# A mixture of experts in f32 with weights loaded once per expert, in place of f16 pairs loaded per block

## The chip, the core and the metric

The kernel runs on one core of one Trainium2 chip. The metric is the device time of one execution in microseconds; the median over three runs is what kernels are compared by. A profile is one execution of its own.

## What is computed

Sixteen sequences of 64 tokens (D = 256) pass through seven blocks, each with a residual sum: cross-attention to 16 x 256 context rows, self-attention, a mean over eight experts, cross-attention again, a diagonal state-space layer, and then a layer of its own attention and a mixture of eight experts. The change touches that mixture:

```python
h = h + moe(rms_norm(h, norm2_w), router_w, router_b, W1, b1, W2, b2, W3, b3)
...
logits = x @ router_w + router_b
topv, topi = jax.lax.top_k(logits, TOP_K)          # TOP_K = 2
topw = jax.nn.softmax(topv, axis=-1)
h1 = jnp.einsum('bsd,edf->ebsf', x, W1) + b1       # 8 x 256 x 1024
h2 = jnp.einsum('bsd,edf->ebsf', x, W2) + b2
h = h2 * jax.nn.silu(h1)
eo = jnp.einsum('ebsf,efd->ebsd', h, W3) + b3      # 8 x 1024 x 256
out = jnp.einsum('bse,ebsd->bsd', comb, eo)
```

All inputs are f32.

## The kernel before

Every engine has its own hand-written program, and they wait for each other on semaphores. The stages follow one another in the order ln, xa0, sa, ffn, xa1, ssm, rope, la, moe. The cross-attentions (`cross`, 16 steps and 4 to drain) keep K, V and scores of one sequence each; `inner` (sa and la) runs over 8 tiles of 128 tokens with 4 steps to drain. x, its normed copy and its transpose stay in SBUF. The weights of the stages lie in one buffer, `arena`, which the expert stage later uses as a ring of three slots (`ring`).

**Splitting the experts' weights.** A f32 value is kept as a pair of f16, high and low part. The 8 experts have 96 pieces of 128x512. For each, SP loads the piece (L401), POOL copies it to f16 (L1249) and subtracts that copy from the piece (L1250), and SP stores both parts in the DRAM tensor `w_parts` (L407, `pass_piece`). `split_piece` stands in POOL's steps of sa, ffn, xa1 and la, two pieces a step (one in most steps of la). In xa1, SP passes two pieces and then loads the context of the sequence after next (`load_context`, L372), in one queue.

**Tokens.** In la each normed tile (DVE, L1662) is split in the same way: ACT writes the high part (L1101), POOL the low part (L1316). DVE's norm of the next tile waits for `row_lo`. The router (L1807 to L1849) sorts the 2048 pairs of token and expert into 23 blocks of 128 rows, so that every block has one expert, `owner[b]`; spare blocks get the last one. POOL scatters the tiles' rows with 16 indirect transfers to `x_rows` (L1403).

**Experts.** For each block b, SP reads `owner[b]` (L434) and loads that expert's 3 MB of pairs into `ring[b % 3]` (L436) and its biases (L438), as soon as the sum of block b - 3 is done. PE turns the rows (L938), and multiplies weights (stationary) with tokens (moving, 128 columns) into `S`, feature by row. Each product is three f16 products, high x high, high x low, low x high (L489 to L491, `split_product`): 96 for the hidden layer, 24 of 256 columns for `down`. ACT applies silu with the bias as a column (L1197, 8 of 128 columns), DVE adds the second bias and multiplies (L1880) and splits the result (L1887, L1889). `down` of block b - 1 follows `hidden` of block b. ACT takes the sums, SP stores them to `y_rows` (L459). After the last block POOL fetches the rows back (L1409), and DVE adds them to x.

```python
            for b in range(BLOCKS):
                sp.wait_ge(summed, b + 1)
                if b + RING < BLOCKS:
                    load_weights(b + RING)
```

## Time and profile before

| | us |
|---|---|
| median of 3 runs | 1152.88 (1151.72 to 1153.59) |
| profiled execution | 1152.05 |
| its span, first to last instruction | 1150.2 |
| PE busy | 842.4 (73%) |
| PE weight load busy | 692.3 (60%) |
| DVE busy | 613.4 (53%) |
| ACT busy | 477.1 (41%) |
| POOL busy | 394.1 (34%) |
| mean granted PE clock | 0.855 of 2.4 GHz |

1.9 us of the profiled execution lie outside the span. Busy time alone does not say what sets the time: the stages have different limits, so each is read by itself, by which wait ends last in it. The stages lie about here in the span: xa0 28 to 214, sa to 317, ffn to 420, xa1 to 618, ssm and rope to 697, la to 811, routing and scatter to 855, experts to 1123, gathering and output to 1150.

### The profile page before, as it was taken

Reading aid. Unit: us, or ns where it says so; the run is one execution under the profiler, and the core shown is the slowest. Engines: PE = TensorE matmul, PEld = TensorE weight load, DVE = VectorE, ACT = ScalarE, POOL = GpSimd, SP = SyncE. Lnnn points to the kernel's source line nnn. Section 1 sums busy time; section 2 is a strip of 40 time slices with the busy share of each in tenths; the row PEclk is TensorE's granted clock in tenths of the full one; section 3 lists DMA queues with packets and bytes.
Section 4 is the critical chain, followed back from the end, with each engine's and each line's share of the span. In section 5 each row is a group of like instructions: output and inputs, shape, how many; then the busy total and the mean of one; then the engine's idle time right before and its main releaser. Section 6 shows DMA issues by size and latency. Waiting matters only on the chain.

```text
span 1150.2 us, 25357 instructions
## 1 busy us (share of the span) xinstructions
PE 842.4 (73%) x8692; PEld 692.3 (60%) x8692; DVE 613.4 (53%) x1647; ACT 477.1 (41%) x1715; POOL 394.1 (34%) x577
## 2 busy tenths in 40 slices
PE   2898898699578878988875635775548887688880
PEld 1666665588448766666654514563438877677870
DVE  2477777578546745565563765764314434334342
ACT  1565665356427645565651013664003222222220
POOL 3355655534457453344336323223340000000005
PEclk9999999889789989999995657876558888888885
DMA  7111114523323344334324002111287778887754
GB/s 304 47 47 55 46 46 152 188 76 112 111 73 129 103 135 138 101 102 146 117 74 146 0 0 93 38 38 53 66 326 283 264 264 304 301 303 257 261 208 114
DMA packets 90183, 161.63 MB, mean 141 GB/s; under 512 B 9841, under 2 KB 23921, under 8 KB 89329
## 3 DMA queue, kind: packets, MB, share of 16 engines
q1 hardware_dynamic: 88560, 156.30, 39.5%
q0 software_dynamic: 1536, 4.20, 1.2%
q8 instruction: 53, 0.87, 0.3%
q14 instruction: 34, 0.27, 0.1%
HBM read 126.12 MB, written 34.34 MB: 140 GB/s over the span
## 4 chain that ended last, share of the span: by engine, by line
PE 38%; DVE 14%; ACT 14%; DMA 14%; issue 9%; POOL 8%; SPq 1%; DVEq 1%; POOLq 0%; ACTq 0%; another core or an unknown queue 0%
DMA kbuf<-in_b 11%; ACT probs L1088 5%; PE ps L489 4%; PE ps L490 4%; PE ps L491 4%; PE ps L820 4%; PE ps L526 3%; ACT probs L1047 3%; PE ps L569 3%; PE ps L585 2%; DVE stat L1426 2%; DMA ctx_t<-in_ctx 2%; ACT probs L1038 2%; PE ps L538 2%; PE ps L618 1%
## 5 line engine op out<-in xcount | busy, mean ns | idle before, releaser
L489 PE MATMUL ps<-qbuf,arena 128*128 128x128 f16 x736 | 148.3, 240 | 50.7 <-DMA kbuf<-in_b 50.1
L490 PE MATMUL ps<-qbuf,arena 128*128 128x128 f16 x736 | 148.1, 240 | 0.0
L491 PE MATMUL ps<-qbuf,arena 128*128 128x128 f16 x736 | 147.5, 240 | 0.0
L1880 DVE SCALAR_TENSOR_TENSOR probs<-ps,kbuf,ctx_t 128x128 f32<-128x128 f32 x184 | 51.8, 345 | 172.9 <-ACT ctx_t L1197 172.9
L1218 POOL TENSOR_TENSOR var<-mv,half 128x1 f32<-128x1 f32 x64 | 12.6, 196 | 312.2 <-DVE mv L1427 226.0
L1197 ACT ACTIVATE ctx_t<-ps,kbuf 128x128 f32<-128x128 f32 x184 | 52.6, 368 | 153.6 <-PE ps L491 153.6
L1250 POOL TENSOR_TENSOR piece_out<-piece_in,piece_out 128x512 f16<-128x512 f32 x96 | 113.2, 1179 | 7.7
L489 PEld LDWEIGHTS ps<-qbuf,arena 128*128 128x128 f16 x736 | 80.7, 110 | 52.8 <-DMA kbuf<-in_b 51.9
L1409 POOL DMA_INDIRECT pt<-y_rows,neg x16 | 15.3, 959 | 280.0 <-DMA y_rows<-vbuf 275.4
L1275 POOL TENSOR_TENSOR probs<-probs,gp 128x512 f32<-128x512 f32 x64 | 81.4, 1304 | 52.3 <-ACT probs L1038 52.3
L569 PE MATMUL ps<-pack_const,probs 128*128 128x128 f32 x512 | 77.4, 288 | 28.8 <-DVE vbuf L1468 11.3
L569 PEld LDWEIGHTS ps<-pack_const,probs 128*128 128x128 f32 x512 | 57.7, 145 | 52.9 <-DVE vbuf L1468 13.1
L491 PEld LDWEIGHTS ps<-qbuf,arena 128*128 128x128 f16 x736 | 80.8, 110 | 0.0
L490 PEld LDWEIGHTS ps<-qbuf,arena 128*128 128x128 f16 x736 | 80.6, 110 | 0.0
L526 PE MATMUL ps<-ctx_t,arena 128*128 128x256 f32 x256 | 66.3, 404 | 7.7 <-DMA ctx_t<-in_ctx 5.5
L1249 POOL CAST piece_out<-piece_in 128x512 f16<-128x512 f32 x96 | 60.0, 625 | 34.1 <-DMA piece_in<-in_w 32.8
L1475 DVE COPY pt<-ps 128x512 f32<-128x512 f32 x64 | 44.3, 692 | 47.6 <-PE ps L569 47.5
L1038 ACT ACTIVATE probs<-probs,mx 128x256 f32<-128x256 f32 x128 | 63.2, 496 | 12.6 <-DVE mx L1500 12.6
L538 PE MATMUL ps<-arena,ctx_t 128*128 128x256 f32 x256 | 63.5, 390 | 0.0
L1047 ACT ACTIVATE probs<-ps,mx 128x256 f32<-128x256 f32 x128 | 58.7, 492 | 8.7 <-DVE mx L1511 8.7
L820 PE MATMUL ps<-xt_all,arena 128*128 (+1 forms) x512 | 61.2, 282 | 0.0
L526 PEld LDWEIGHTS ps<-ctx_t,arena 128*128 128x128 f32 x256 | 48.3, 199 | 20.8 <-issue 13.0
(229 smaller groups left out, 2085.2 us busy)
## 6 DMA issues: line engine op xcount, KB each, us to landing
arena<-w_parts SPq DMA_DIRECT2D x23, 3072.0 KB, 10.7
piece_in<-in_w SPq DMA_DIRECT2D x96, 256.0 KB, 2.8
w_parts<-piece_out SPq DMA_DIRECT2D x96, 256.0 KB, 2.1
ctx_t<-in_ctx SPq DMA_DIRECT2D x32, 256.0 KB, 2.7
x_rows<-piece_out SPq DMA_DIRECT2D x1, 2944.0 KB, 16.7
qbuf<-x_rows SPq DMA_DIRECT2D x23, 128.0 KB, 9.4
y_rows<-vbuf SPq DMA_DIRECT2D x23, 128.0 KB, 9.7
arena<-in_xa SPq DMA_DIRECT2D x2, 1282.0 KB, 7.2
```

What stands on the lines that cost most here:

```text
L489: pe.matmul(dst, a[0], b[0], start=first, stop=False)
L490: pe.matmul(dst, a[0], b[1], start=False, stop=False)
L491: return pe.matmul(dst, a[1], b[0], start=False, stop=final)
L526: last = pe.matmul(AB[:, hf * KEYS:(hf + 1) * KEYS], wk[:, k, hf * P:(hf + 1) * P], c[:, k, :], start=k == 0, stop=k == DC - 1)
L538: last = pe.matmul(AB[:, 512 + kt * D:512 + (kt + 1) * D], c[:, k, kt * P:(kt + 1) * P], wv[:, k, :], start=k == 0, stop=k == DC - 1)
L569: last = pe.transpose(AB[:, o:o + P], pr[:, 2 * c + n, kt * P:(kt + 1) * P], ident)
L820: last = pe.matmul(S[:, o:o + P], we[:, k, e, hh * P:(hh + 1) * P], XT[:, k, bass.ts(i, P)], start=k == 0, stop=k == DC - 1)
L1038: act.activation(p, p, ACT.Exp, bias=mx[:, s * HEADS + n:s * HEADS + n + 1], scale=-1.0, accum_out=ssum[:, s * HEADS + n:s * HEADS + n + 1])\
L1047: last = act.activation(probs[:, s * 2048 + n * KEYS:s * 2048 + (n + 1) * KEYS], S[:, o:o + KEYS], ACT.Exp, bias=mx[:, s * HEADS + n:s * H ...
L1249: chain.link(pool.tensor_copy(both[:, 0:PIECE], src))
L1250: pool.tensor_tensor(both[:, PIECE:], src, both[:, 0:PIECE], ALU.subtract).then_inc(piece_split, 1)
L1275: pool.tensor_tensor(p, p, gw, ALU.mult).then_inc(g["weighted"].sem, 1)
```

## The change

- The experts are computed in f32 from the input's own weights. Piece splitting, `w_parts`, `row_parts` and `split_product` go; POOL's and ACT's splitting of tiles in la goes, and DVE writes the normed tile into `kept_rows`.
- Each expert's 3 MB are loaded once: three after the arena's stages end (two when xa1's last residual is done, one after la), the other five each when the last block of the expert three before has been summed (L413 there reads the count of blocks from a table, `ends_of`).
- The tokens are the stationary operand (`block_x`), the weights the moving one, 512 columns wide. PE finds the slot by two register reads a block (`find_weights`), from `owner` and a new table `place_of`, which DVE computes in the routing.
- The biases come first, by a product of a 0/1 matrix `choice` (made by DVE) with the table of biases, in four groups of 32 rows.
- The hidden layer now comes out as rows; ACT and DVE gate 512 columns at a time, PE turns the result in 8 transposes (`turn_hidden`), ACT and DVE copy it. `down` lags by two blocks.
- ACT issues the row loads and the stores of sums, which SP did.

```diff
-PIECE = 512
-PIECES = DC * 2 * FF // PIECE + FT * D // PIECE
+EXPERT = DC * 2 * FF + FT * D
...
-        ring = [arena[:, i * PIECES * PIECE:(i + 1) * PIECES * PIECE].bitcast(F16).rearrange("p (j n) -> p j n", j=PIECES)
-                for i in range(RING)]
-        piece_in = sb("piece_in", 2 * PIECE)
-        piece_out = sb("piece_out", 4 * PIECE, F16)
+        ring = [arena[:, i * EXPERT:(i + 1) * EXPERT] for i in range(RING)]
+        zeros = sb("zeros", D)
+        kept_rows = [probs[:, (1024, 3072)[i % 2] + (i // 2) * D:(1024, 3072)[i % 2] + (i // 2 + 1) * D] for i in range(TILES)]
...
-        turned_rows = [ps[:, o:o + 256].bitcast(F16) for o in (3072, 3584)]
-        block_sums = [ps[:, o:o + D] for o in (2048, 2560)]
+        turned_rows = [M[:, i * D:(i + 1) * D] for i in range(2)]
+        block_sums = [C[:, i * D:(i + 1) * D] for i in range(2)]
...
-                load_piece(c + 2)
+            def load_expert(e):
+                sp.dma_start(ring[e % RING], t["w"][e, :, :]).then_inc(weights_in[e % RING], 16)
...
-            for c in range(LA_PIECES, EXPERTS * PIECES):
-                pass_piece(c)
-
-            for s in range(2):
-                sp.wait_ge(piece_stored[s], 16 * EXPERTS * PIECES // 2)
+                         zeros[:, :].unsqueeze(1).broadcast_to([BLOCK, BLOCKS, D])).then_inc(cleared, 16)
+            for k in range(2, SEQS):
+                load_context("xa1", k, k % 2)
+
+            hold(sp, G["xa1"]["resid"], TILES)
+            load_expert(0)
+            load_expert(1)
+            for e in range(RING):
+                sp.wait_ge(weights_in[e], 16)
+                sp.sem_inc(weights_ready, 1)
             sp.wait_ge(routed, 2)
...
             def turn_block(b):
                 pe.wait_ge(rows_in[b % AHEAD], 16 * (b // AHEAD + 1))
-                if b >= 2:
-                    pe.wait_ge(x_taken, b - 1)
+                if b >= 1:
+                    pe.wait_ge(x_taken, b)
+                for k in range(DC):
+                    last = pe.transpose(turned_rows[b % 2][:, k * P:(k + 1) * P],
+                                        block_rows[:, b % AHEAD, k * P:(k + 1) * P], ident)
...
+            def find_weights(b):
+                e = pe.value_load(owner[0:1, b:b + 1], min_val=0, max_val=EXPERTS - 1)
+                at = pe.value_load(place_of[0:1, b:b + 1], min_val=0, max_val=(RING - 1) * EXPERT)
+                return e, arena[:, bass.ds(at, EXPERT)]
+
+                pe.wait_ge(chosen_, b + 1)
+                if b >= 1:
+                    pe.wait_ge(silued, 2 * b)
+                    pe.wait_ge(gated_done, 2 * b)
+                for j in range(4):
+                    r = slice(32 * j, 32 * j + 32)
+                    pe.matmul(S[:, j * 512:(j + 1) * 512], choice[r, b % 2, :], w["b12"][r, :],
+                              start=True, stop=False, skip_group_check=True)
                 pe.wait_ge(x_taken, b + 1)
-                xt = [[block_x[:, b % 2, (2 * part + k) * P:(2 * part + k + 1) * P] for k in range(DC)]
-                      for part in range(2)]
+                pe.wait_ge(weights_ready, e + 1)
+                for j in range(4):
+                    for k in range(DC):
+                        o = (j * 2 + k) * 512
+                        last = pe.matmul(S[:, j * 512:(j + 1) * 512], block_x[:, b % 2, k * P:(k + 1) * P],
+                                         weights[:, o:o + 512], start=False, stop=k == DC - 1, skip_group_check=True)
+                    if j % 2 == 1:
+                        last.then_inc(hidden_done, 1)
+
...
-            def down(b):
-                pe.wait_ge(hid_done, 2 * (b + 1))
-                if b >= 2:
-                    pe.wait_ge(out_taken, b - 1)
...
+            def down(b, weights):
+                pe.wait_ge(ht_act, b + 1)
                 for f in range(FT):
-                    j, at = 8 + f // 2, (f % 2) * D
+                    o = 4096 + f * D
+                    last = pe.matmul(block_sums[b % 2], hidden_cols[:, b % 2, f * P:(f + 1) * P], weights[:, o:o + D],
+                                     start=f == 0, stop=f == FT - 1)
+                last.then_inc(G["blocks"]["summed"].sem, 1)
...
-                    down(b - 1)
+                    held[b] = find_weights(b)
+                    hidden(b, *held[b])
+                if 1 <= b <= BLOCKS:
+                    turn_hidden(b - 1)
+                if b >= 2:
+                    down(b - 2, held[b - 2][1])
...
+            def load_rows(b):
+                act.dma_start(block_rows[:, b % AHEAD, :], x_rows[b * BLOCK:(b + 1) * BLOCK, :])\
+                   .then_inc(rows_in[b % AHEAD], 16)
...
+                if b + AHEAD < BLOCKS:
+                    load_rows(b + AHEAD)
...
-
+                act.wait_ge(out_taken, b + 1)
+                act.dma_start(y_rows[b * BLOCK:(b + 1) * BLOCK, :], block_out[:, b % 2, :])\
+                   .then_inc(out_stored[b % 2], 16)
...
-                    act.wait_ge(weights_in[b % RING], 32 * (b // RING + 1))
-                        if f % 4 == 0:
-                            act.wait_ge(hidden_done, 2 * b + f // 4 + 1)
-                        act.activation(gated[:, f * BLOCK:(f + 1) * BLOCK],
-                                       S[:, (f // 4) * 1024 + (f % 4) * P:(f // 4) * 1024 + (f % 4 + 1) * P], ACT.Silu,
-                                       bias=block_bias[:, b % RING, f:f + 1]).then_inc(silued, 1)
+                    act.wait_ge(hidden_done, 2 * b + 1)
+                    for hf in range(2):
+                        if b >= 1:
+                            act.wait_ge(gated_done, 2 * b - 1 + hf)
+                        r = slice(hf * 512, (hf + 1) * 512)
+                        act.activation(gated[:, r], S[:, r], ACT.Silu).then_inc(silued, 1)
+                if 1 <= b <= BLOCKS:
+                    act.wait_ge(h_turned, 2 * b - 1)
+                    if b >= 3:
+                        hold(act, G["blocks"]["summed"], b - 2)
+                    act.activation(hidden_cols[:, (b - 1) % 2, 0:512], AB[:, 0:512], ACT.Copy).then_inc(ht_act, 1)
+                if b >= 2:
...
-                src = piece_in[:, s * PIECE:(s + 1) * PIECE]
-                chain.link(pool.tensor_copy(both[:, 0:PIECE], src))
-                pool.tensor_tensor(both[:, PIECE:], src, both[:, 0:PIECE], ALU.subtract).then_inc(piece_split, 1)
...
-                    if live(k, 4, TILES) and st == "la":
-                        i = k - 4
-                        hold(pool, g["row_hi"], i + 1)
-                        own = row_parts[i % 2][:, (i // 2) * 2 * D:(i // 2 + 1) * 2 * D]
-                        pool.tensor_tensor(own[:, D:], xn[:, :], own[:, 0:D], ALU.subtract).then_inc(g["row_lo"].sem, 1)
...
                             hold(dve, g["rstd"], k - 2)
-                            hold(dve, g["row_lo"], k - 3)
-                            dve.scalar_tensor_tensor(out=xn[:, :], in0=tile(xn_all, k - 3), scalar=rstd[:, :],
+                            dve.scalar_tensor_tensor(out=kept_rows[k - 3], in0=tile(xn_all, k - 3), scalar=rstd[:, :],
...
+            def choose_biases(b):
-                    dve.tensor_tensor(lo[:, r], product[:, r], hi[:, r], ALU.subtract).then_inc(hid_done, 1)
+                    dve.wait_ge(hidden_done, 2 * b - 2)
+                dve.tensor_scalar(choice[:, b % 2, :], owners[:, b:b + 1].broadcast_to([P, P]), K["lane"], None,
...
+                    dve.wait_ge(hidden_done, 2 * b + 2)
+                    for hf in range(2):
+                        dve.wait_ge(silued, 2 * b + hf + 1)
+                        if b >= 2:
+                            dve.wait_ge(h_turned, 2 * b - 3 + hf)
+                        r = slice(hf * 512, (hf + 1) * 512)
+                        dve.tensor_tensor(hidden_rows[:, b % 2, r], S[:, 1024 + hf * 512:1024 + (hf + 1) * 512], gated[:, r],
+                                          ALU.mult).then_inc(gated_done, 1)
+                if b >= 1:
+                    dve.wait_ge(h_turned, 2 * b)
+                    if b >= 3:
+                        hold(dve, G["blocks"]["summed"], b - 2)
+                    dve.tensor_copy(hidden_cols[:, (b - 1) % 2, 512:1024], AB[:, 512:1024]).then_inc(ht_dve, 1)
 
 
             weights = wgt[:, 16:32].rearrange("p (r t) -> p r t", r=2)
@@ -1936,6 +1896,7 @@
     c["iota"] = np.tile(np.arange(24), (P, 1))
     c["steps"] = np.tile(BLOCK * np.arange(8), (P, 1))
```

How it moves instructions. In the three listings a row is line, operation, output, inputs and shape, with what it waits for behind it; a count stands at the end.

SP in xa1, before: two pieces between one context load and the next.

```order
L372 DMA ctx_t<-in_ctx 128x512 [waits v_projected]
L407 DMA w_parts<-piece_out 128x1024 [waits piece_split]
L401 DMA piece_in<-in_w 128x512 [waits piece_split]
L407 DMA w_parts<-piece_out 128x1024 [waits piece_split]
L401 DMA piece_in<-in_w 128x512 [waits piece_split]
L372 DMA ctx_t<-in_ctx 128x512 [waits v_projected]
```

and now, from the clearing of `x_rows` to the experts' first loads:

```order
L398 DMA x_rows<-zeros 128x23x256 [waits made]
L366 DMA ctx_t<-in_ctx 128x512 [waits v_projected] x14
L392 DMA arena<-in_w 128x6144 [waits resid]
L392 DMA arena<-in_w 128x6144
L392 DMA arena<-in_w 128x6144 [waits xt]
```

The context loads stand behind nothing but each other.

POOL in a step of la, before (`var` and `rstd` are the root of the mean square):

```order
L1218 TENSOR_TENSOR var<-mv,half 128x1 [waits squared]
L1219 TENSOR_TENSOR rstd<-var,half 128x1 [waits pool_chain]
L1310 TENSOR_TENSOR x<-x,xn_all 128x256
L1316 TENSOR_TENSOR probs<-xn,probs 128x256 [waits row_hi]
L1249 CAST piece_out<-piece_in 128x512 [waits piece_loaded1,piece_stored1]
L1250 TENSOR_TENSOR piece_out<-piece_in,piece_out 128x512 [waits pool_chain]
```

and now:

```order
L1204 TENSOR_TENSOR var<-mv,half 128x1 [waits squared]
L1205 TENSOR_TENSOR rstd<-var,half 128x1 [waits pool_chain]
L1273 TENSOR_TENSOR x<-x,xn_all 128x256
```

Nothing of the low part and of the pieces is left.

PE in the expert stage, now, from the end of one block's down products to the next block's hidden products (`neg` holds the tables, `obuf` the choice, `qbuf` the tokens):

```order
L940 MATMUL ps<-arena,pt 128x256
L895 MATMUL ps<-pack_const,qbuf 128x128 [waits block_x,rows_in5]
L895 MATMUL ps<-pack_const,qbuf 128x128
L900 TENSOR_LOAD neg
L900 ISA x2
L901 TENSOR_LOAD neg
L901 ISA x2
L912 MATMUL ps<-pack_moe,obuf 128x512 [waits block_gated,block_silu,block_chosen]
L912 MATMUL ps<-pack_moe,obuf 128x512 x3
L915 REGISTER_ALU [waits block_x]
L919 ISA [waits weights_ready]
L919 MATMUL ps<-arena,qbuf 128x512
```

The two register reads are new to this queue; the gate of the block before is waited for behind them, at the bias products.

## Rows read from the trace of the kernel before

**Rows 1.** Busy: stretch, length, PE, PEld, DVE, ACT, POOL, clock, DMA share, GB/s
```profile
855.30:1122.60 267.30, 216.19 (x2852) 207.35 (x2852) 103.22 (x276) 73.70 (x231) 0.00 (x0) 0.86 0.76 270
883.70:895.30 11.60, 9.95 (x115) 9.76 (x116) 3.55 (x11) 2.29 (x8) 0.00 (x0) 0.71 0.88 318
```

**Rows 2.** Expert stage by line: count, busy us, mean ns, idle before, releasers
```profile
L489 PE MATMUL ps<-qbuf,arena 128*128 128x128 f16 x736 | 148.3, 240 | 50.7 <-DMA kbuf<-in_b 50.1 <-ACT qbuf L1180 0.4 <-DVE probs L1880 0.2
```

**Rows 3.** DMA issues (count, size, median us to landing); chain (start, us)
```profile
arena<-w_parts SPq DMA_DIRECT2D x23, 3072.0 KB, 10.7
...
1088.58 12.48 DMA kbuf<-in_b
```

**Rows 4.** Timeline, PE at 998 us, f16 with 256 columns (start, duration in us)
```profile
998.41 0.27 PE L490 MATMUL ps<-arena,pt 128*128 128x256 f16 x1
998.51 0.27 PE L491 MATMUL ps<-arena,pt 128*128 128x256 f16 x1
```

**Rows 5.** PE with 512 f32 columns: timeline at 321 us; records of that line
```profile
321.56 1.02 PE L778 MATMUL ps<-xt_all,arena 128*8 128x512 f32 x2
...
L778 PE MATMUL ps<-xt_all,arena x8: 592/833/1057, 317.3 to 322.0; 128*8 128x512 f32 x8
```

**Rows 6.** Timeline, PE, 505 to 511 us, second cross-attention
```profile
505.56 0.71 PE L585 MATMUL ps<-kbuf,qbuf 32*128 32x256 f32 x8
506.21 1.09 PE L569 MATMUL ps<-pack_const,probs 128*128 128x128 f32 x8
...
509.55 1.99 PE L526 MATMUL ps<-ctx_t,arena 128*128 128x256 f32 x8
511.47 0.32 PE L608 MATMUL ps<-pt,vbuf 128*32 128x128 f32 x4
```

**Rows 7.** Records of one line: copy of 512 columns on DVE (min/median/max ns)
```profile
L1475 DVE COPY pt<-ps x64: 691/692/693, 46.7 to 607.9; 128x512 f32<-128x512 f32 x64
```

**Rows 8.** Records of one line: SP's read of the owner table
```profile
L434 SPq TENSOR_LOAD <-neg x23: 262/275/503, 827.2 to 1095.5; - x23
L434 SPq FUSED_REGOPS  x23: 152/152/173, 827.7 to 1095.9; - x23
```

**Rows 9.** xa1: PE's waits (us in total, times, longest); busy; chain
```profile
PE ps L526 <- DMA ctx_t<-in_ctx: 4.7, 6, 0.9
...
486.70:509.20 22.50, 19.97 (x182) 14.49 (x182) 13.27 (x24) 13.20 (x45) 8.85 (x12) 1.00 0.35 117
...
518.28 3.12 DMA ctx_t<-in_ctx
```

**Rows 10.** la: DVE's waits (us in total, times, longest); timeline, 765 us
```profile
DVE xn L1662 <- POOL probs L1316: 17.3, 7, 4.8
...
764.79 0.55 POOL L1219 TENSOR_TENSOR rstd<-var,half 128x1 f32<-128x1 f32 x1
765.31 0.73 POOL L1310 TENSOR_TENSOR x<-x,xn_all 128x256 f32<-128x256 f32 x1
765.99 0.67 POOL L1316 TENSOR_TENSOR probs<-xn,probs 128x256 f16<-128x256 f32 x1
...
766.79 0.70 DVE L1662 SCALAR_TENSOR_TENSOR xn<-xn_all,rstd,arena 128x256 f32<-128x256 f32 x1 [2.10 <-POOL probs L1316]
```

**Rows 11.** Timeline, DVE at 354 us, first tile of the expert mean
```profile
354.63 0.41 DVE L1431 TENSOR_SCALAR xn<-x,mv,rstd 128x256 f32<-128x256 f32 x1 [0.52 <-POOL rstd L1219]
```

**Rows 12.** Timeline, last scatter and first row loads
```profile
848.58 0.97 POOL L1403 DMA_INDIRECT x_rows<-probs,neg  x1 [0.30 <-issue]
...
853.13 3.65 SPq L441 DMA_DIRECT2D qbuf<-x_rows  x8
```

**Rows 13.** Timeline, DVE at 260 us; page, POOL's two split operations
```profile
260.27 0.54 DVE L1431 TENSOR_SCALAR xn<-x,mv,rstd 128x256 f32<-128x256 f32 x1
...
L1250 POOL TENSOR_TENSOR piece_out<-piece_in,piece_out 128x512 f16<-128x512 f32 x96 | 113.2, 1179 | 7.7
L1249 POOL CAST piece_out<-piece_in 128x512 f16<-128x512 f32 x96 | 60.0, 625 | 34.1 <-DMA piece_in<-in_w 32.8
```

More of the change, by code:

```diff
@@ L974, in _ @@
+            pe.wait_ge(routed, 2)
             turn_block(0)
-            for b in range(BLOCKS + 1):
+            held = {}
+            for b in range(BLOCKS + 2):
                 if b + 1 < BLOCKS:
@@ L1367, in ffn_step @@
                         root_of_variance(G["ffn"], k - 1)
-                    for j in range(2):
-                        split_piece(j, k + INNER_STEPS)
                     chain.restart()
@@ L1396, in _ @@
                 inner("la")
[L1398 removed]
+            hold(pool, G["la"]["normed"], TILES)
             pool.wait_ge(cleared, 16)
```

228 lines of the change are left out of this document (70 added, 158 removed).

## The prediction

> **What bounds the kernel now.** I read the page first, then the busy time of each engine by stretch, then the chain of waits, then the timeline inside each loop that the diff touches. The expert stage runs from the first turned rows at 855.3 us to the last product at 1122.6 us: 267.3 us for 23 blocks, 11.6 us a block. PE is busy 216 us of it, DMA engines 76% of it [rows 1]. The PE group of the hidden products is preceded by 50.7 us of idle time, 50.1 of them ended by the loads of a block (the small bias load is the last of the pair that PE waits for) [rows 2]. A block's weights are 3 MB and land 10.7 us after issue; in the chain such a load stands as one piece of 12.5 us every second block [rows 3]. So transfers set the stage's pace, and PE, at 0.10 to 0.11 us for an f16 product of 256 columns [rows 4], waits for them; in every second block its granted clock falls to a mean of 0.71, between the two levels 2.4 and 1.2 GHz [rows 1]. The change removes the loads per block, so what counts is how long a block takes PE in f32.
>
> **PE's block after the change.** An f32 product shows as two matmul records: the code's four products at L526 are eight records. With 512 columns at full clock two records take 1.02 us from start to end, and the last alone 0.59, so the step is 0.43 us [rows 5]. With 256 columns the step should be half, 0.216: the eight records of L526 start at 509.55 and the next group at 511.47, 1.92 us = 8 x 0.216 + 0.2, so a change from one group to another costs 0.1 to 0.2 us. Eight transposes take 1.09 us from the first start to the last end; I take 1.0 up to the next group. L585 is four products side by side in four row groups: 0.65 us from start to the next group's start, so two rounds of 0.216 and 0.2 [rows 6]. A block then takes:
> - hidden layer, 8 products of 512 columns: 16 x 0.43 + 0.1 = 7.0
> - bias products, four row groups, 512 columns, in L585's manner: 2 x 0.43 + 0.2 = 1.1
> - 8 transposes of the gated rows and 2 of the tokens: 1.0 + 0.3 = 1.3
> - down, 8 products of 256 columns: 16 x 0.216 + 0.2 = 3.7
>
> Sum 13.0 us, of which nothing runs beside anything else on PE. Times 23 it is 299 us. Its lower bound, with no cost for changing groups, is 12.3 us (283); its upper bound takes 0.24 per 256 columns, the mean of L526 with its group change, throughout: 7.7 + 1.3 + 1.3 + 3.9 = 14.2 (327). I take the middle, since the long chains of 16 have one change each.
>
> **What could hold PE up inside a block.** After the hidden products PE has 8 transposes, the down products of two blocks ago and 2 transposes before it needs the gate: 1.0 + 3.7 + 0.3 = 5.0 us. The gate is two silus of 512 columns on ACT, the first of which can start half a hidden layer earlier, and two products of 512 columns on DVE; a DVE copy of that size out of PSUM takes 0.69 [rows 7]. That is some 1.6 us behind the last hidden product, hidden by 5.0. Only in the first two blocks is that cover missing: 1.4 and 0.5 us. ACT also gets both row transfers; at 0.43 us of issue each on SP and four to five more operations of 0.4 to 0.7 it has some 4 us of work in 13. Each expert's weights arrive once. With the reference's router on the drawn inputs the blocks per expert are 3, 1, 3, 4, 2, 3, 2, 2, and three spare blocks go to the last; a slot comes free at least two blocks (26 us) ahead of its next use and a 3 MB load takes 10.7 [rows 3], so no load should show. PE without waits should hold the 2.4 GHz level; the first 4.5 us ran at half clock before and will again, which costs 2.3 us here. Stage: 299 + 2.3 + 1.9 = 303, against 267.3: **+36 us**.
>
> **New on PE's queue:** two register reads a block, at the place right ahead of the bias products, for which PE's trace of before has no row. The nearest is SP's read of the same table: the first starts at 827.2, and its second part, 0.15 long, at 827.7, so 0.65 us a read [rows 8]. Two of them are 1.3 us, 30 us over 23 blocks, if the array stands still meanwhile; nothing if the sequencer reads them while the array works off what is queued. It can: the last condition that it waits for ahead of the reads is met soon after the hidden products of the block before begin, and the next thing that it needs behind them, that block's gate, comes some 3 us before the array gets there. The other end of the cost is 30. I take 0, because in the loops register work stands in PE's order between L585 and L569 and costs the array nothing: the one ends at 506.27, the other has begun at 506.21 [rows 6], and keep 30 for the range. The Trainium skill, "DMA: Bandwidth & Descriptors", section "Latency and other measured facts", gives a register load from memory a floor of about 600 ns; by it alone the sum would be 2 x 0.6 x 23 = 28 us longer. The page "TensorE: Matmul & The Clock Gate", section "Architectural detail: the array is 16× 32×32, not 1× 128×128", gives PE a queue of 64 instructions, which would cover the reads, since some 52 stand between them and the hidden layer's end; no row here shows its depth.
>
> **Ahead of the stage.** (1) Second cross-attention: SP passes two pieces through POOL before it loads the next context. PE waits for the context 6 times, 4.7 us; a pair of sequences takes 22.5 us, PE is busy 20.0 of it, and the chain goes POOL's split, store, load, context of 3.1 us [rows 9]. With the pieces gone the context is loaded as soon as its slot is free: -4.5 us; at most the whole idle 2.5 us of seven pairs, -17. (2) Last attention: DVE's norm of a tile waits for POOL's low part of the tile before, 7 times; rstd ends at 765.34, then POOL adds (0.73) and subtracts (0.67), and DVE starts only at 766.79 [rows 10]. Now it waits for rstd alone: 1.45 us x 7 = -10; bounds -7 (ACT's sixteen exponentials next) and -12. (3) First tile of the expert mean: POOL splits two pieces ahead of its rstd, but DVE had been free only 0.52 us [rows 11]: -0.5. In the first inner attention POOL's splits lie beside ACT's exponentials: 0. (4) Routing and entry: six more small DVE operations ahead of the slots, +1; the scatter's last transfer took 4.5 us from issue beside two weight loads, -1.5 now; ACT issues eight row loads (3.65 us on SP) before it takes the first rows, +1 [rows 12]. Together +0.5. The tail after the last sum is the same.
>
> **Sum** against the profiled execution, 1152.05 us (the median of the three runs is 1152.88, 0.8 more): +36 - 4.5 - 10 - 0.5 + 0.5 = +21.5, so 1173.5.
>
> **Rivals.** (A) The register reads stop the array. For it: it is two serial reads in PE's own order; against it: the gapless loops. +30: 1203. (B) Faster: POOL stops sharing DVE's way to memory. The same norm operation took 0.54 us on DVE while POOL split a piece, and 0.41 while it did not [rows 11, 13]. POOL's splits are 173 us of work in all [rows 13]; if DVE, slowed by a quarter during them, set the pace of all those loops, 43 us would go, and the kernel would take 1152 + 36 - 43 - 10 + 0.5 = 1135. It decides once more than 21 us of that lies on the path. Against it: those loops' chains run through PE and ACT, and most of DVE's reads there are of PSUM. (C) A stall of some other kind in the block loop, of a microsecond a block (ACT's two transfer issues, a late slot, a clock that falls): 1196.
>
> **How the numbers follow.** Forecast 0.64, A 0.20, B 0.05, C 0.08, no difference 0.03. Likeliest 1173.5. The forecast's own range is 1158 (12.3 us a block) to 1190; with A and C it reaches 1206. Under it lie B and the far end of the first cross-attention gain. About 0.2% (2.3 us) is what a measurement of this kernel tells from no change. Faster 0.05, same 0.03, slower 0.92.
>
> **What would show it.** A period of 13.0 us from one block's bias products to the next, at clock 1.0, with PE idle nearly nowhere and DMA under a fifth; no wait of L526 for a context; DVE's norm in the last attention ended by rstd; a stretch of about 303 us from turned rows to the last sum. Wrong, if PE shows a gap of about 1.3 us ahead of every bias group (A), if its records of 512 columns are not 0.43 apart, or if idle time on PE is ended by silus or weights.

## The result and the profile after

| | before | after |
|---|---|---|
| median of 4 runs, us | 1152.95 (1151.72 to 1153.59) | 1160.45 (1158.43 to 1163.12) |
| profiled execution, us | 1152.05 | 1158.43 |
| its span, us | 1150.2 | 1156.4 |
| mean granted clock | 0.855 | 0.890 |

The changed kernel takes 1.0068 times as long, 95% interval 1.0045 to 1.0091: slower by 7.5 us. The forecast was 21.5 us slower. Direction and range hold; the size does not.

The page of the kernel after, the busy times and the core's line of PE and clock by fortieths of the span:

```profile
span 1156.4 us, 21443 instructions
PE 915.1 (79%) x6990; PEld 652.1 (56%) x6990; DVE 539.9 (47%) x1469; ACT 459.0 (40%) x1592; POOL 216.5 (19%) x376
PE   2899897799578878999966447765499999999990
PEclk9999999789779989999976667865599999999996
```

The expert stage is the run of nines in the last quarter of PE's line (the 30th to the 39th fortieth). In [rows 1] PE had 216 us of work in 267. Now, busy time by stretch, for the whole stage and for one block of it:

```profile
core 0: us, PE busy (x) PEld busy (x) DVE busy (x) ACT busy (x) POOL busy (x), PEclk, DMA share, GB/s
829.40:1129.30 299.90, 294.81 (x1150) 171.29 (x1150) 47.57 (x90) 57.56 (x116) 0.00 (x0) 0.99 0.20 72
906.00:918.68 12.68, 12.68 (x55) 7.42 (x51) 2.08 (x4) 2.45 (x6) 0.00 (x0) 1.00 0.64 258
```

PE is 98% busy at 2.4 GHz, and the transfers are down to a fifth. The wait of [rows 2] is gone. The chain of waits of the kernel after over two blocks (start, length, what) is PE alone:

```profile
904.99 1.07 PE ps L912 x8
906.06 7.06 PE ps L919 x16
913.13 0.88 PE ps L930 x8
914.00 3.46 PE ps L940 x16
917.46 0.22 PE ps L895 x2
917.67 1.07 PE ps L912 x8
918.75 7.06 PE ps L919 x16
```

L912 is the bias products, L919 the hidden products, L930 the transposes of gated rows, L940 the down products, L895 the transposes of the tokens. The block is 12.68 us (forecast 13.0). There is no gap of 1.3 us ahead of L912.

**Where the other microseconds are.** I cut both traces at the same instructions (the last record of a line, or the first where a stage begins) and took the lengths between the cuts. Each column is one profiled execution, and such lengths scatter also where nothing differs. From the last scores of the first cross-attention to the last scores of the first inner attention the changed kernel took 93.2 us and the one of run 7, which is the same up to the last stage, 89.8.

| stretch, us | before | after | difference | forecast |
|---|---|---|---|---|
| start to the first product of the expert mean | 336.3 | 336.6 | +0.3 | 0 |
| expert mean, to DVE's last add | 79.1 | 73.2 | **-5.9** | -0.5 |
| second cross-attention, to its last product | 198.2 | 190.4 | **-7.8** | -4.5 |
| state-space stage | 59.6 | 59.1 | -0.6 | 0 |
| rope | 23.9 | 21.5 | **-2.4** | 0 |
| last attention, to the router's first product | 113.6 | 105.4 | **-8.3** | -10 |
| routing, slots, scatter, to the first turned rows | 44.6 | 43.3 | -1.3 | +0.5 |
| expert stage | 267.6 | 299.9 | **+32.3** | +36 |
| behind the last sum | 27.2 | 27.1 | -0.2 | 0 |

The sum is +6.2 us of span. So 3.7 us of the error lie in the expert stage, and the rest ahead of it: more was freed there than was forecast.

Part of this goes with the granted clock. The expert mean in the kernel before, the changed one, and those of runs 5 and 6 below (run 5 is the kernel before with one transfer moved, run 6 the changed kernel with an edit in the last stage only):

```profile
336.25:415.39 79.14, 65.69 (x539) 63.21 (x537) 54.73 (x140) 58.22 (x136) 45.73 (x100) 0.96 0.32 104
336.55:409.75 73.20, 62.81 (x539) 60.25 (x537) 41.98 (x140) 59.60 (x136) 15.74 (x66) 1.00 0.00 1
337.50:415.90 78.40, 65.20 (x539) 61.94 (x538) 56.07 (x140) 57.34 (x136) 45.32 (x100) 0.98 0.32 107
335.60:410.60 75.00, 64.59 (x539) 61.89 (x537) 41.93 (x140) 59.74 (x136) 15.32 (x66) 0.98 0.00 1
```

With the pieces and at a mean clock of 0.98 the stage took 78.4 us, without them and at the same clock 75.0 (74.9 to 75.0 in runs 3, 6 and 7). So some 3.4 of the 5.9 us are there at a like clock; the other 2.5 go with a clock of 1.00 against 0.96. Whether the pieces also brought the clock down, or how it fell was chance, no run separates. The second cross-attention took 192.1 us in runs 3, 6 and 7 (mean clock 0.95) where the table has 190.4 (0.96). A microsecond or two of a single row is therefore not yet an effect.

The clearest place is still the expert mean. Its adds on DVE, before and after (groups of instructions in the expert mean: busy us, mean ns, idle before):

```profile
L1723 DVE TENSOR_TENSOR scratch<-scratch 128x128 f32<-128x128 f32 x112 | 45.4, 436 | 18.5 <-ACT scratch L1134 15.8
```
```profile
L1671 DVE TENSOR_TENSOR scratch<-scratch 128x128 f32<-128x128 f32 x112 | 32.8, 294 | 26.6 <-ACT scratch L1106 24.6
```

The same 112 adds took 436 ns each and now take 294. Nothing about them has changed but what runs beside them: POOL's splits of the pieces and the pieces' transfers are gone (run 1 tells the two apart). Rope shows it with single instructions. The timeline of the kernel before (start, length), four products of DVE at L1787 beside POOL's L1249 and L1250:

```profile
692.40 1.21 POOL L1250 TENSOR_TENSOR piece_out<-piece_in,piece_out 128x512 f16<-128x512 f32 x1
692.63 3.10 DVE L1787 TENSOR_TENSOR scratch<-rot,pack_const 128x128 f32<-128x128 f32 x4
...
693.55 0.67 POOL L1249 CAST piece_out<-piece_in 128x512 f16<-128x512 f32 x1
...
694.30 1.28 POOL L1250 TENSOR_TENSOR piece_out<-piece_in,piece_out 128x512 f16<-128x512 f32 x1
```

and the same four of the kernel after:

```profile
678.45 0.90 DVE L1735 TENSOR_TENSOR scratch<-rot,pack_const 128x128 f32<-128x128 f32 x4
```

3.10 us against 0.90: this is nearly all of the 2.4 us of rope. These pieces belong to the first steps of the last attention, in which POOL has nothing else to wait for: it starts on them while DVE is still in rope. The forecast had no term for that.

### The profile page after: what moved, and what is told of

It reads as the page before. It is cut to its first block, busy times and chain, and to the rows that moved or that the text cites. A ratio compares the mean times of both kernels' runs of the same rounds, so it can differ in the third digit from the quotient of the medians.

```text
span 1156.4 us, 21443 instructions
## 1 busy us (share of the span) xinstructions
PE 915.1 (79%) x6990; PEld 652.1 (56%) x6990; DVE 539.9 (47%) x1469; ACT 459.0 (40%) x1592; POOL 216.5 (19%) x376
## 4 chain that ended last, share of the span: by engine, by line
PE 55%; ACT 16%; DVE 15%; issue 7%; POOL 5%; DMA 2%; DVEq 1%; ACTq 0%; POOLq 0%; SPq 0%; another core or an unknown queue 0%
PE ps L919 14%; PE ps L940 7%; ACT probs L1063 5%; ACT probs L1022 5%; PE ps L779 3%; PE ps L484 3%; PE ps L527 3%; PE ps L543 3%; PE ps L912 2%; DVE stat L1375 2%; ACT probs L1013 2%; PE ps L930 2%; PE ps L496 2%; ACT pt L1002 2%; PE ps L506 1%
## 5 line engine op out<-in xcount | busy, mean ns | idle before, releaser
L919 PE MATMUL ps<-arena,qbuf 128*128 x368 | 164.8, 601 | 0.0
L1843 DVE TENSOR_TENSOR probs<-ps,ctx_t 128x512 f32<-128x512 f32 x46 | 29.6, 686 | 253.4 <-PE ps L919 253.4
L919 PEld LDWEIGHTS ps<-arena,qbuf 128*128 128x128 f32 x368 | 68.4, 191 | 95.6 <-issue 95.6
L1204 POOL TENSOR_TENSOR var<-mv,half 128x1 f32<-128x1 f32 x64 | 12.7, 199 | 493.7 <-DVE mv L1376 387.0
L940 PE MATMUL ps<-arena,pt 128*128 x368 | 83.4, 380 | 0.7 <-ACT vbuf L1163 0.7
L940 PEld LDWEIGHTS ps<-arena,pt 128*128 128x128 f32 x368 | 68.1, 190 | 9.4 <-issue 1.1
L1181 ACT ACTIVATE ctx_t<-ps 128x512 f32<-128x512 f32 x46 | 25.0, 594 | 90.4 <-PE ps L919 90.4
L1106 ACT ACTIVATE scratch<-ps,bec,counts 128x128 f32<-128x128 f32 x128 | 56.3, 458 | 4.9 <-PE ps L779 4.1
L779 PEld LDWEIGHTS ps<-xt_all,arena 128*128 128x128 f32 x512 | 57.9, 192 | 0.2
L1002 ACT ACTIVATE pt<-ps 128x512 f32<-128x512 f32 x64 | 38.9, 607 | 44.3 <-PE ps L527 44.3
L496 PEld LDWEIGHTS ps<-arena,ctx_t 128*128 128x128 f32 x256 | 46.3, 189 | 10.9 <-issue 5.6
```

What stands on the lines that cost most here:

```text
L496: last = pe.matmul(AB[:, 512 + kt * D:512 + (kt + 1) * D], c[:, k, kt * P:(kt + 1) * P], wv[:, k, :], start=k == 0, stop=k == DC - 1)
L779: last = pe.matmul(S[:, o:o + P], we[:, k, e, hh * P:(hh + 1) * P], XT[:, k, bass.ts(i, P)], start=k == 0, stop=k == DC - 1)
L919: last = pe.matmul(S[:, j * 512:(j + 1) * 512], block_x[:, b % 2, k * P:(k + 1) * P], weights[:, o:o + 512], start=False, stop=k == DC - 1 ...
L940: last = pe.matmul(block_sums[b % 2], hidden_cols[:, b % 2, f * P:(f + 1) * P], weights[:, o:o + D], start=f == 0, stop=f == FT - 1)
L1002: act.activation(pt32[:, s * 2048 + c * 512:s * 2048 + (c + 1) * 512], AB[:, 0:512], ACT.Copy)\
L1106: act.activation(out, S[:, (n % 4) * 512:(n % 4) * 512 + P], ACT.Relu, bias=bec[:, n:n + 1], scale=counts[:, n // 2:n // 2 + 1]).then_inc( ...
```

## The experiments

**1. POOL's splits put back, without transfers.** Theory O (order) says that all gains ahead of the stage come from waits; theory S (sharing) says that POOL's work slows DVE.

```diff
+            def split_spare(s):
+                both = spare_out[:, s * 1024:(s + 1) * 1024]
+                chain.link(pool.tensor_copy(both[:, 0:512], spare_in[:, :]))
+                chain.mark(pool.tensor_tensor(both[:, 512:], spare_in[:, :], both[:, 0:512], ALU.subtract))
```

> The changed kernel with POOL's splits put back at their old places (two a step in the first inner attention, the expert mean and the second cross-attention, sixteen in the last attention: 96 casts and 96 subtractions of 512 columns), on a spare tile of ones, with no transfer around them. Theory O (order): what was gained ahead of the expert stage came from waits on transfers and on the low part of a row, and POOL's arithmetic costs DVE nothing: 1160 us, and the expert mean still ends 5.6 us earlier than before. Theory S (sharing): POOL's splits slow DVE's operations that read two operands from SBUF. DVE's add of 128 columns in the expert mean took 436 ns before and 294 ns after; with the splits back it goes to some 430 again and the expert mean is 5 to 6 us longer; in the second cross-attention part of the 7.8 us comes back, in the last attention little: 1167 to 1174 us.

Measured: 1173.17 us, 1.0168 times the kernel before (1.0147 to 1.0189), 12.7 us over the changed kernel. Theory S. The expert mean is 79.2 us long at a mean clock of 0.96, as before the change (79.1 at 0.96), and rope 24.2. The second cross-attention is 190.6, as in the changed kernel: nothing of its gain was sharing. In the last attention the splits cost 0.8 us. DVE's adds in this kernel's expert mean:

```profile
L1688 DVE TENSOR_TENSOR scratch<-scratch 128x128 f32<-128x128 f32 x112 | 46.2, 443 | 17.1 <-ACT scratch L1108 14.5
```

**2. Only the casts on POOL.**

```diff
-                chain.mark(pool.tensor_tensor(both[:, 512:], spare_in[:, :], both[:, 0:512], ALU.subtract))
```

> The changed kernel with only the 96 casts of 512 columns on POOL (no subtractions). With both, DVE's two-operand adds in the expert mean took three times as long when they began during a POOL instruction, which they seem to sit out. If any POOL instruction does this, casts too: adds that begin during a cast take 0.5 us or more, against 0.29, and the expert mean is 1 to 2 us longer than in the changed kernel. If only POOL's two-operand instruction does it, all adds take 0.29 and the expert mean is 73 to 75 us as there.

Measured: 1158.71 us (one run), expert mean 73.6 us:

```profile
L1687 DVE TENSOR_TENSOR scratch<-scratch 128x128 f32<-128x128 f32 x112 | 36.9, 338 | 23.0 <-ACT scratch L1108 21.2
```

A cast holds DVE up as well: the 19 adds that began during one took 556 ns on average, the others 293. But a cast is half as long, and what is left of it was mostly absorbed: the stage is only 0.4 us longer, at the same mean clock of 1.00. The expected 1 to 2 us did not come there; rope went from 21.5 to 22.6 us. So the price is not the slower DVE but what of it lies on the path: 4 us more DVE time cost 0.4 us of the expert mean, 13 us cost 3.4 at a like clock and 6 with the lower one.

**3. The row's high and low part and the wait for the low one put back.**

```diff
+                        pool.tensor_tensor(own[:, D:], kept_rows[i], own[:, 0:D], ALU.subtract).then_inc(g["row_lo"].sem, 1)
...
+                            hold(dve, g["row_lo"], k - 3)
```

> The changed kernel with the row's high and low parts made again in the last attention (ACT's copy, POOL's subtraction, into a spare tile) and with DVE's norm waiting for the low part of the tile before. Theory O: this wait is the whole 8.3 us that the last attention gained, so it comes back: 1168 us (1.0 to 1.2 us a tile, seven times). Theory S: a part of the 8.3 us was the sixteen splits on POOL, which are not put back here: 1164 to 1166 us.

Measured: 1167.14 us, ratio to before 1.0115 (1.0085 to 1.0145). The last attention is 112.0 us to the router, 6.6 over the changed kernel. The DVE waits of the last attention, kernel after and this one (us, times, longest):

```profile
DVE probs L1610 <- POOL rstd L1205: 10.1, 6, 3.7
```
```profile
DVE probs L1621 <- POOL spare_rows L1284: 16.5, 7, 4.9
```

Of the 8.3 us this is 6.6, and the splits of run 1 are 0.8; 0.9 stays unassigned.

**4. The same wait moved in the kernel before**, by giving the normed row two tiles:

```diff
-                            hold(dve, g["row_lo"], k - 3)
-                            dve.scalar_tensor_tensor(out=xn[:, :], in0=tile(xn_all, k - 3), ...
+                            hold(dve, g["row_lo"], k - 4)
+                            dve.scalar_tensor_tensor(out=tile(rot2, (k - 3) % 2), in0=tile(xn_all, k - 3), ...
```

> The kernel before with the normed row of the last attention in two alternating tiles, so that DVE's norm waits for the low part of the tile before last instead of the last; copies, subtractions and pieces all stay. The run with the row parts put back gave the wait 6.6 us, and the sixteen splits 0.8. If the wait alone is the cost, this kernel gains 6 to 7: 1146 us. If POOL's own work in its order is the cost (its subtraction and splits delay its next rstd), it gains under 2.

Measured: 1148.44 us, ratio 0.9969 (0.9948 to 0.9990); the last attention goes from 113.6 to 109.1 us. That is 4.5 us, between the two theories: two thirds of what the wait cost. DVE's 17.3 us of waits for the low part are gone from its list, and 8.5 us of waits for rstd stand in their place. rstd stands on POOL behind the subtraction and the splits that this kernel still makes. That this order causes the missing 2 us is argued, not shown.

**5. The contexts ahead of the pieces, in the kernel before.**

```diff
+                if k + 2 < SEQS:
+                    load_context("xa1", k + 2, k % 2)
                 pass_piece(XA1_PIECES + 2 * k)
                 pass_piece(XA1_PIECES + 2 * k + 1)
-                if k + 2 < SEQS:
-                    load_context("xa1", k + 2, k % 2)
```

> The kernel before with one thing moved: in the second cross-attention SP loads the next context ahead of the two pieces of its step instead of behind them; pieces and splits all stay. If the 6 to 8 us that this attention gained by the change came from the order on SP (the prediction's cause), nearly all of it shows here: 1145 to 1148 us, no wait of PE for a context. If it came from the pieces being gone (POOL's work, or the transfers beside it), nothing: 1152 to 1154.

Measured: 1146.35 us, ratio 0.9961 (0.9943 to 0.9979). The second cross-attention goes from 198.2 to 192.1 us, and the wait for a context ([rows 9]: 4.7 us, 6 times) is gone from PE's list. 192.1 is also what runs 3, 6 and 7 took, which have no pieces at all, so the order of two lines on SP explains the whole gain. The 1.7 us more of the changed kernel's profiled execution go with its clock, 0.96 against 0.95. How large the gain is, is less sure than the 6.1 us of two executions: the ratio stands for 4.5 us (2.4 to 6.6), and the kernel of run 8, which has the old order, took 195.1 us at a clock of 0.97, 4.7 more than the changed one.

**6. and 7. The register reads: none, and six instead of two.**

```diff
-                e = pe.value_load(owner[0:1, b:b + 1], ...)
-                at = pe.value_load(place_of[0:1, b:b + 1], ...)
+                e = (0, 0, 0, 1, 2, 2, 2, 3, 3, 3, 3, 4, 4, 5, 5, 5, 6, 6, 7, 7, 7, 7, 7)[b]
```
```diff
+                for again in range(4):
+                    pe.value_load(place_of[0:1, b:b + 1], ...)
```

> The changed kernel with PE's two register reads per block taken out: expert number and place of the weights are constants that hold for the drawn tokens. Theory of the prediction: the reads lie beside queued work, the block stays at 12.68 us and the time at 1160. Rival A, in whatever part: each read that holds the array gives 0.65 us back a block, so a block of 12.0 or 11.4 us and 1145 or 1131 us.

> The changed kernel with six register reads per block on PE instead of two. If a read takes 0.65 us of PE's sequencer, six take 3.9 us; the chain of queued work between the last thing awaited and the first product behind them is about 7 us of hidden products and 1 us of transposes. The prediction's theory: still hidden, or just at the edge: 12.7 to 13.5 us a block, 1160 to 1178. Rival A (a read stops the array): at least 4 x 0.65 us more a block, 15.3 us, 1220 us.

Measured (one run each): without reads 1160.14 us and a stage of 299.3 (299.9 with two), and 12.68 us from block to block in both: beside queued work two reads cost nothing. With six, 1167.65 us and a stage of 308.6. The chain of that kernel:

```profile
904.87 0.43 PE ps L921
905.30 0.87 PE ps L932 x8
906.17 3.46 PE ps L942 x16
909.63 0.22 PE ps L895 x2
909.84 0.16 issue
910.00 1.14 PE ps L914 x8
911.14 7.06 PE ps L921 x16
```

In the middle of the stage four more reads make the block 0.26 us longer (12.94), not 4 x 0.65 = 2.6, and the gap shows where the prediction looked for it, ahead of the bias products. So PE reads ahead of the array; two reads are hidden, six no longer quite. Ahead of the first block's bias products nothing long is queued, and there the reads show. PE's timeline at that place with two reads, with six and with none:

```profile
833.12 2.09 PE L912 MATMUL ps<-pack_moe,obuf 32*128 32x512 f32 x8 [0.93 <-issue]
836.46 2.09 PE L914 MATMUL ps<-pack_moe,obuf 32*128 32x512 f32 x8 [3.50 <-issue]
834.68 2.09 PE L911 MATMUL ps<-pack_moe,obuf 32*128 32x512 f32 x8
```

The four more reads cost 3.50 - 0.93 = 2.57 us here, 0.64 each: the price per read of rival A was right (0.65), and only its condition, that nothing covers it, fails from the second block on. This one place holds 2.6 of the 8.7 us between the two stages. Rival A is out for this kernel.

**8. The f16 pairs kept, the experts loaded once.** If transfers were what held the stage before, removing them alone should pay.

```diff
-                pe.wait_ge(weights_in[b % RING], 32 * (b // RING + 1))
+                pe.wait_ge(weights_ready, e + 1)
...
-                                wt = [ring[b % RING][:, j, part * PIECE + at:part * PIECE + at + P] for part in range(2)]
+                                wt = [weights[:, (2 * j + part) * PIECE + at:(2 * j + part) * PIECE + at + P] for part in range(2)]
```

> The kernel before with f16 pairs kept and only the loading changed: each expert's split weights are loaded once, PE picks slot and expert by a register, the biases of all blocks are loaded ahead, ACT issues the rows and sums. Before, PE had 50 us of waits in the stage, and half clock in part of it. 96 f16 products of 128 columns at 0.055 (half of the 0.109 of 256 columns), 24 of 256 columns at 0.108 and four transposes are 8.1 us a block. Theory of the prediction (transfers set the stage before): 8.0 to 9.4 us a block, stage 185 to 220 instead of 267, 1070 to 1105 us. Rival (a block is bound by the chain from the products through silu, gate and split, or by weight loads into the array of 110 ns for each 128 columns): 10.5 us a block or more, over 1125 us.

Measured: 1167.45 us, ratio 1.0142 (1.0102 to 1.0182). A miss: the stage is 286 us, longer than the 267.6 that waited for transfers. PE's timeline, before and here:

```profile
874.48 0.22 PE L489 MATMUL ps<-qbuf,arena 128*128 128x128 f16 x1
874.53 0.22 PE L490 MATMUL ps<-qbuf,arena 128*128 128x128 f16 x1
874.59 0.22 PE L491 MATMUL ps<-qbuf,arena 128*128 128x128 f16 x1
874.64 0.22 PE L489 MATMUL ps<-qbuf,arena 128*128 128x128 f16 x1
```
```profile
938.17 0.23 PE L494 MATMUL ps<-qbuf,arena 128*128 128x128 f16 x1 [0.62 <-issue]
938.23 0.22 PE L495 MATMUL ps<-qbuf,arena 128*128 128x128 f16 x1
938.29 0.23 PE L496 MATMUL ps<-qbuf,arena 128*128 128x128 f16 x1
938.42 0.23 PE L494 MATMUL ps<-qbuf,arena 128*128 128x128 f16 x1
```

Three products began within 0.17 us; now they need 0.25 (938.17 to 938.42), of which the last step alone takes 0.12, and the reads show as a gap of 0.62 us. Two suspects: the register in the address, or something that loading once brought with it.

**9. The same with constants for the registers.** (They hold for the drawn tokens only: the kernel leaves out PE's choice of the expert.)

```diff
-                return e, arena16[:, bass.ds(at, EXPERT)]
+                return e, arena16[:, at:at + EXPERT]
```

> The kernel with f16 pairs loaded once per expert, with slot and expert as constants (they hold for the drawn tokens) where it had read them into registers. With registers the block took 12.4 us: a product whose stationary operand's address is in a register began 124 ns after the one before, against 56 ns at L489 to L491 of the kernel before, and PE stood still 0.6 to 0.8 us ahead of a block's first product. Theory R (register addresses of a stationary operand, and reads with nothing queued ahead of them, make the block long): 56 ns throughout, no gap, 8.0 to 8.6 us a block, stage 185 to 200, time 1070 to 1085 us. Rival L (loading once has changed something else: the clock, the loads' place, ACT's new transfers): pace and block stay, 12 us, 1160 us.

Measured: 1077.53 us (one run), stage 193.6 us, 8.4 a block. Theory R. The two stages, registers and constants:

```profile
851.80:1137.80 286.00, 266.91 (x2852) 213.72 (x2852) 103.34 (x276) 76.28 (x231) 0.00 (x0) 0.99 0.23 77
```
```profile
854.90:1048.50 193.60, 191.38 (x2852) 184.24 (x2852) 103.29 (x276) 76.29 (x231) 0.00 (x0) 0.99 0.33 113
```

The same 2852 products at the same clock: 92 us are the price of the registers, read and used as the address of a stationary operand, among short products. (The expectation's 124 ns hold for one step in three only; the hidden products began 88 ns apart on average, against 56.) Whether it is the stationary operand or the shortness of the products that makes the address dear stays open: no run has short products with a moving operand addressed by a register, or long ones with a stationary one. And the block loads of the kernel before had cost 267.6 - 193.6 = 74 us, in waits and in a clock of 0.86 against 0.99.

**10. Pairs as the moving operand.** The changed kernel's scheme, whose registers cost nothing, with the f16 products:

```diff
+                        for n, (px, pw) in enumerate(((0, 0), (0, 1), (1, 0))):
+                            last = pe.matmul(S[:, j * 512:(j + 1) * 512], block_x[:, b % 2, px, k * P:(k + 1) * P],
+                                             weights[:, o + pw * 512:o + pw * 512 + 512], start=False,
+                                             stop=k == DC - 1 and n == 2, skip_group_check=True)
```

> A candidate that should beat both kernels: the changed kernel (weights moving, loaded once per expert, picked by a register, f32 rows, biases by a product), but with the weights as f16 pairs as before (POOL's splits and their transfers are back, contexts loaded ahead of them), and with tokens and gated rows split where they are copied out of PSUM (ACT the high, DVE the low part). Per block: bias products 1.07, 24 f16 products of 512 columns at 0.215 (half of 0.43) 5.2, transposes 0.87 and 0.31, 24 of 256 columns at 0.109 2.6: 10.0 us instead of 12.68. Theory R: a register-addressed moving operand costs nothing (in the kernel with pairs loaded once the down products kept 109 ns), so 10.0 to 10.4 us a block, stage 230 to 240 us; ahead of it the splits cost what they did in the run with the splits back, first turned rows at 842 to 846; in all 1103 to 1118 us. Rival (any register address costs some 65 ns a product, or ACT and DVE with their five more operations set the block): 12 us a block or more, 1145 us or more.

Measured: 1111.18 us, ratio 0.9638 (0.9625 to 0.9652). The block is 10.07 us, PE without a gap from the fourth block on. The stage is 241.1, 9.5 more than 23 such blocks; half of this is that its first 9.7 us run at half clock.

**11. The same with f16 biases and a shorter entry.**

```diff
+            chain.link(dve.tensor_copy(bias_hi[:, :], w["b12"]))
+            chain.link(dve.scalar_tensor_tensor(out=bias16[:, :], in0=bias_hi[:, :], scalar=K["part"], in1=w["b12"],
+                                                op0=ALU.mult, op1=ALU.add))
...
-            for b in range(AHEAD):
+            for b in range(2):
                 load_rows(b)
             take_rows(0)
+            for b in range(2, AHEAD):
+                load_rows(b)
```

> The candidate with f16 pairs as moving operand, with two more edits. (1) The bias products also in f16: the biases' high parts in rows 0 to 7 of each group of 32, the low parts in rows 8 to 15, made by two DVE operations, and a choice of ones in both, so four products side by side in one pass instead of two f32 passes: 1.07 us a block becomes about 0.3 (0.215 and a group change of 0.1). (2) ACT issues two row loads, takes the first rows, and then issues the other six: in the candidate before, eight issues of 0.45 us stood in the chain of waits ahead of the first rows. If the array's time is the sum of its products (a block was 10.07 us without a gap, PE 100% busy), the block falls to 9.3 and the entry by 2 to 3 us: 23 x 0.75 + 2.5 = 20 us less, 1089 to 1095. If instead ACT and DVE are near the pace (their gate and copies behind the last product, 1.3 us of gate and two waits), less of it shows: a block of 9.7 or more, over 1100.

Measured: 1091.41 us, ratio 0.9469 (0.9448 to 0.9489): 61 us faster than the kernel before and the fastest here that does not rest on the drawn tokens. The stage is 221.9 us, and in its chain the hidden products recur every 9.33 us:

```profile
935.83 5.29 PE ps L957 x24
941.12 0.87 PE ps L969 x8
941.99 2.62 PE ps L979 x24
945.16 5.29 PE ps L957 x24
```

## Why the prediction was right and wrong

**Right: the bound.** The stage went from transfers to PE, and the block is the sum of its products at the pace read from other loops. Run 6 shows that the register reads are not in it. That the time lies in the range, 1158 to 1190, is in part luck: the lower end stood for a block of 12.3 us, but the block took 12.68, and the other microseconds were gained ahead of the stage.

**The expert stage, +36, measured +32.3.** The forecast's pieces were 7.0 + 1.1 + 1.3 + 3.7 = 13.0; the trace has 6.97 + 1.07 + 1.18 + 3.46 = 12.68. The pace was exact: 0.43 and 0.216 us. What was too large are the group changes: 0.2 us were added to the down products and 0.1 to the transposes, read off groups of different shapes at L526 and L585, and in the block they cost nothing. Only the change to and from products in row groups shows: the step from the last transpose to L912 is 0.20 us where such a step is 0.11, and the steps from L912 on are up to 0.1 longer than 0.43. Times 23 the block's 0.32 is 7.4 us, of which a slower start took half back: the stage is 8.3 us longer than 23 blocks of 12.68, where the forecast had 2.3 + 1.9. PE waits 1.43 us for ACT's copy of the first rows, which stands behind ACT's eight row loads, and 0.93 us for the reads, and the clock is at its lower level for the first 7.3 us, where 4.5 were taken.

**Rival A, register reads: rightly set at nothing.** The page "DMA: Bandwidth & Descriptors" of the Trainium skill (section "Latency and other measured facts"), taken as a serial cost, would have added 28 us; runs 6 and 7 show that the array doesn't wait for two reads. The size itself agrees: 0.64 us for each read that stood uncovered in run 7. Setting it at nothing was right for all blocks but the first, because 7 us of long products are queued ahead. In run 8, with short ones, the same reads left a gap of 0.6 us.

**The second cross-attention, -4.5, measured -7.8.** The cause was right: run 5 has the gain from the order on SP alone. The term was the sum of PE's waits for contexts, 4.7 us, and it was near: at a like clock the gain is 4.7 to 6.1 us, and 1.7 of the 7.8 go with the clock of the one profiled execution. The prediction's other end was -17.

**The last attention, -10, measured -8.3.** Cause right (run 3: 6.6 us). 1.45 us were taken for each of seven tiles; DVE's own waits for rstd (10.1 us after, 0.4 before) took over a part.

**The failed step is term (3), the first tile of the expert mean at -0.5 us, and beside it rope at nothing.** The prediction looked there for a wait on POOL's rstd, found half a microsecond, and stopped. What POOL cost was in the length of DVE's own instructions, and a list of waits doesn't show it. Rival B had the mechanism and a fair "against it: most of DVE's reads there are of PSUM", but it was priced as one sum over all stages, 43 us or nothing, with a chance of 0.05. Taken stage by stage, that sentence would have given the answer: PSUM readers are safe, so look for the loops in which DVE reads two operands from SBUF. These are the 112 adds of the expert mean, whose mean of 436 ns, with undisturbed ones at 290, stood in the trace, and the products of rope. The first inner attention, set at 0 as well, has such instructions too (the eight of L1618 took 12.0 us in all before and 9.8 after); whether they count there is lost in the scatter of that stretch. Run 1 puts 2.7 us in rope and 6.0 in the expert mean, the latter with the lower clock (4.2 against runs 3 and 6). The two rows together, 7.8 us beyond the forecast, are half of its error of 15 us; at a like clock of the expert mean they are 5.3.

**Routing and entry, +0.5, measured -1.3.** The slots took 1.0 us more, as said; scatter and row loads together took 2.3 us less, where the forecast had 0.5 (1.5 for the scatter, less 1 for ACT's issues). The two chains of waits, before and after, show where:

```profile
848.58 4.53 DMA x_rows<-probs,neg
```
```profile
824.79 2.42 DMA x_rows<-probs,neg
```

The last scatter lands 2.1 us sooner. ACT's issues are not in this stretch: they show in the 1.43 us for which PE waits at the start of the expert stage.

## What to carry to other kernels

When a change takes work off an engine that seems idle enough, compare, stage by stage, the mean duration of the neighbours' instructions with their shortest: the difference is what that engine may cost them, and no list of waits has it. When you compare a stage between two profiles, compare its granted clock first. Price the parts of a change separately before you accept its total: here loading once was worth 74 us (with constants in place of registers), and f32 in place of f16 pairs cost 59 in the changed kernel's own scheme (241.1 to 299.9); the one change held both. If a register must address an operand, try it with a long moving one before the stationary one of short products.

## What was not expected of the hardware

- **A POOL instruction holds up DVE's instructions with two SBUF operands until it ends.** In the kernel before, the 29 adds at L1723 that began during a split took 858 ns on average (1251 at most), the 68 beside which no split ran 290; the split had 792 ns to go on average. 27 of the 29 ended 139 to 152 ns after the split did; the two that began right with one took 293. The 15 adds that were under way when a split began took 284. The nine normalisations (L1431, one tile and two columns of scalars) that began during a split ended 146 to 148 ns behind it too, 573 ns long, against 409 with POOL idle. DVE instructions reading PSUM showed nothing: 346 against 347, 336 against 343 and 692 against 687 ns at L1630, L1626 and L1468. ACT's relus beside the splits of run 1 stayed at 457 against 459 ns.
- **Registers in an address are free or dear.** f32 products of 512 and 256 moving columns kept 0.43 and 0.216 us with the moving operand addressed by a register, f16 ones of 256 columns 0.109. f16 products of 128 columns whose stationary operand a register addresses need 0.25 us for three, against 0.17 with constants; which of the two, the operand's role or the product's length, decides is open.
- **A stage at 2.4 GHz need not be shorter.** The granted clock went from 0.86 to 0.99 in the expert stage, and the stage grew by 32 us: the lower clock had been a sign of waiting, and f32 fills the array for longer than the waits had lasted.
